# Python-unrolled loops of a four-stage transformer kernel turned into hardware loops

## The reference

```python
x = x + xattn0(ctx, ctx, layernorm(x))        # softmax over ctx·normed x, applied to ctx
x = x + gated_ffn(layernorm(x))               # NF4 weights, 1024 -> 2752 -> 1024, silu(gate) * up
x = x + pooled_gate(layernorm(x), ctx)        # mask of the top 154 of 256 channels of ctx, pools, conv, sigmoid
x = x + fp8_linear(layernorm(x))              # x and weight rounded to fp8, matmul in f32, bias
```

## Time and profile before

| | us |
|---|---|
| three runs | 1971.41, 1971.42, 1970.74 |
| their median | 1971.41 |
| the profiled execution, its own time | 1971.41 |
| its span, first to last instruction | 1969.6 |
| busy in it: PE, DVE, ACT, POOL | 1716.5, 1822.7, 1206.9, 1080.0 |

### The profile page before, as it was taken

How to read it: one execution, slowest core, us unless ns; L and a number is a source line. 1 busy time by engine, 2 the same in 40 slices (tenths; PEclk the granted TensorE clock), 3 DMA queues, 4 the chain that set the end, 5 groups by cost and what they waited for, 6 DMA issues and landing times. The chain is left out here.

```text
span 1969.6 us, 26301 instructions
## 1 busy us (share of the span) xinstructions
PE 1716.5 (87%) x8581; PEld 867.4 (44%) x8720; DVE 1822.7 (93%) x4424; ACT 1206.9 (61%) x1980; POOL 1080.0 (55%) x835
## 2 busy tenths in 40 slices
PE   6997199999999999999999999999999989432656
PEld 4665044444444444444444444444444443232322
DVE  4886799999999999999999999999999997787997
ACT  2442766666675766666756666667566661495754
POOL 2222666566565665655656656566566560255673
PEclk9999599999999999999999999999999999665778
DMA  8343111111111111111111111111111000221212
GB/s 315 118 137 87 25 19 22 20 27 19 22 25 17 23 22 19 26 20 22 24 18 24 22 19 26 20 22 23 18 24 21 15 13 2 86 65 54 65 43 86
DMA packets 96665, 82.59 MB, mean 42 GB/s; under 512 B 35216, under 2 KB 87184, under 8 KB 96528
## 3 DMA queue, kind: packets, MB, share of 16 engines
q1 hardware_dynamic: 60880, 63.99, 10.1%
q0 software_dynamic: 35648, 16.92, 7.3%
HBM read 74.72 MB, written 23.07 MB: 50 GB/s over the span
## 5 line engine op out<-in xcount | busy, mean ns | idle before, releaser
L713 ACT ACTIVATE b_high_line<-code,b_line_bias 128x512 f32<-128x512 bf16 (+2 forms) x528 | 348.7, 707 | 353.8 <-DVE b_weight L873 353.8
L814 PE MATMUL b_up_ps<-xT_high,b_gate_up 128*128 128x512 bf16 x1344 | 413.5, 379 | 0.0
L814 PE MATMUL b_gate_ps<-xT_high,b_gate_up 128*128 128x512 bf16 x1322 | 403.4, 381 | 0.1
L638 POOL TENSOR_TENSOR b_parts<-b_weight,b_parts 128x512 bf16<-128x512 f32 (+1 forms) x132 | 151.9, 1151 | 415.5 <-ACT b_parts L723 415.5
L713 ACT ACTIVATE b_low_line<-code,b_line_bias 128x512 f32<-128x512 bf16 (+2 forms) x528 | 347.5, 706 | 28.8 <-POOL b_high_line L655 27.3
L932 DVE MATCH_REPLACE8 b_left<-b_best,b_left 128x256 f32<-128x256 f32 x832 | 332.9, 404 | 0.0
L915 DVE MAX8 b_best<-b_left 128x8 f32<-128x256 f32 x832 | 308.7, 409 | 0.2
L814 PE MATMUL b_gate_ps<-xT_low,b_gate_up 128*128 128x512 bf16 x703 | 268.2, 381 | 5.1 <-issue 0.9
L814 PE MATMUL b_up_ps<-xT_low,b_gate_up 128*128 128x512 bf16 x672 | 254.7, 379 | 0.0
L647 POOL TENSOR_TENSOR b_low_line<-b_low_line 128x512 f32<-128x512 f32 (+1 forms) x132 | 187.5, 1420 | 102.2 <-ACT b_low_line L713 101.7
L835 PE MATMUL b_down_ps<-b_down,b_inner_high 128*128 128x512 bf16 (+1 forms) x662 | 210.7, 380 | 0.1
(11 more groups left out here) (154 smaller groups left out, 3044.1 us busy)
## 6 DMA issues: line engine op xcount, KB each, us to landing
x_rows<-in_x_dram SPq DMA_DIRECT2D x8, 1024.0 KB, 5.7
a_ctx<-in_ctx_dram SPq DMA_DIRECT2D x8, 1024.0 KB, 6.9
ctx_t<-a_kT SPq DMA_DIRECT2D x8, 1024.0 KB, 7.1
b_left<-ctx_t SPq DMA_DIRECT2D x64, 128.0 KB, 2.2
mask<-mask_t SPq DMA_DIRECT2D x16, 512.0 KB, 3.8
out_dram<-x_rows SPq DMA_DIRECT2D x8, 1024.0 KB, 4.0
code<-in_L_ffn_gate_codes_dram POOLq DMA_DIRECT2D x42, 128.0 KB, 3.1
code<-in_L_ffn_up_codes_dram POOLq DMA_DIRECT2D x42, 128.0 KB, 2.9
```

The source lines that it names most:

```text
L638: nc.gpsimd.tensor_tensor(parts[j % 2][0:a, 1, 0:n], weight[j % 2][0:a, 0:n], parts[j % 2][0:a, 0, 0:n], ALU.subtract).then_inc(low_made, 1)
L713: ins = nc.scalar.activation((low_line, high_line)[side][i][0:a, 0:n], code[slot][0:a, 0:n], ACT.Relu, bias=line_bias[0:a, side, i:i + 1], ...
L814: ins = nc.tensor.matmul(out, gu_w[b][:, which, wp, k, 0:rows], xT[xp][:, k, tg * HW:(tg + 1) * HW], start=(k == 0 and n == 0), stop=(k == ...
```

## The change

Seven `for` loops of Python, which write a copy of the body per pass, become `Fori` loops, which each engine that takes part runs with an index in a register. `Fori` sets the register, runs the body, adds the step and branches back while the index is under the end. Inside, `c`, `i` and `b` are then no Python integers, so that the thresholds of waits, the slices of X and the addresses of DMAs that depend on them are computed on the engine. `at(m, n)` is false and `there(b)` and `reused(b)` are true in a loop, whose passes are those for which that holds.

```diff
 # attention
         def bodies(eng, body):
             body(0, 0, True, False)
-            for i in range(0, B // 2 - 1):
+            with eng.Fori(0, B // 2 - 1) as i:
                 body(2 * i + 1, 1, True, True)
                 body(2 * i + 2, 0, True, True)
 # attention, SP's loads of X
-            for i in range(0, B // 2 - 1):
+            with sp.Fori(0, B // 2 - 1) as i:
                 for p in range(2):
 # gated_ffn
         def chunks(eng, chunk):
-            for c in range(0, CHUNKS - 2):
+            with eng.Fori(0, CHUNKS - 2) as c:
                 chunk(c)
 # pooled
-            for i in range(1, B // 2 - 1):
+            with eng.Fori(1, B // 2 - 1) as i:
                 body(2 * i, 0)
                 body(2 * i + 1, 1)
 # pooled, SP's loads of masks
-            for i in range(0, B // 2 - 1):
+            with sp.Fori(0, B // 2 - 1) as i:
 # gates_and_fp8_ffn
         def rounds(eng, body):
             body(0, 0)
-            for i in range(0, (B - 4) // 2):
+            with eng.Fori(0, (B - 4) // 2) as i:
                 body(2 * i + 1, 1)
                 body(2 * i + 2, 0)
 # gates_and_fp8_ffn, SP's last stores
-            for b in range(B - 5, B):
+            with sp.Fori(B - 5, B) as b:
                 store(b)
```

## The result

| | us |
|---|---|
| before, four runs in all | 1971.08 median, 1970.19 to 1971.42 |
| after, four runs | 2001.48 median, 2000.66 to 2003.20 |
| after, three more on record | 1998.09, 2000.80, 2002.92 |
| ratio after / before | 1.0153, 95% interval 1.0139 to 1.0168 |
| predicted | 2010, range 1978 to 2042 |

A forecast was written before the change was run, and what follows sets the result against it. PE and DVE, both nearly full in each FFN chunk, were taken to bound the kernel. Taken branches (27.4 us) and register values (11.6 us) added 39.0 us to 1971.41, giving 2010 us, range 1978 to 2042.

The forecast's parts named there:

- Full engines, nothing saved by less code: PE and DVE are within 2 us of full in each FFN chunk; fewer instruction fetches save 0.
- PE fetches the head of its body again (2.4 us a chunk in the sum): At each taken FFN branch PE refetches for 3.1 us, 2.7 showing; with DVE alongside, 2.4 was charged.
- rival (a): PE keeps its body, so DVE's stall counts, less its waits for PE: 26.4 us, 1998 in all; chance 0.20.
- far fewer than 69 packets: Sign on PE's instruction queue q8 that would speak for PE keeping its body through the loop.
- passed five blocks ago, so gone: PE looks ahead about one block, so its body's head, passed five blocks ago, must be fetched again.
- DVE fetches (1.7 us shown): At a taken FFN branch DVE's refetch takes 2.7 us, 1.0 covered by queued adds, so 1.7 show.
- ACT's branch under cover: ACT's 2.7 us branch in the FFN falls into time it waits for DVE, so nothing is charged.
- the number of engine instructions stays as it is: Claim for the whole kernel that arithmetic, tiles, order and number of engine instructions and DMAs do not change.
- Registers, 11.6 us: Values computed in registers where an engine has run dry, all stages: 232 x 0.05 us = 11.6 us.
- Branches of the other stages, 8.2 us: Taken branches outside the FFN: 4.8 us in the first stage, 3.4 in the third and fourth.
- the FFN's branches: Eight taken branches of the FFN loop at 2.4 us each: 19.2 us.

The follow-up runs named there:

- kernel 7: The changed kernel with DVE's FFN back edge hinted and a one-column Silu ahead of ACT's chunk: 1972.25 us, 1.0005 of the kernel before.
- kernel 6: The changed kernel with one more ACT operation, a one-column Silu, at the head of each chunk: 1995.32 us, 1.0121 of the kernel before.

## Why the prediction was right, and where it wasn't

Direction and range held: slower, 2001.5 us in 1978 to 2042. The forecast's 2010 was 8.5 us too high, and its parts were off by more than that, in both directions. So the measured time lies near it partly by luck, as said below.

**Full engines, nothing saved by less code.** Right. DVE's busy time is unchanged, straight chunks still take 131.4 us, and the part of the code that is no longer fetched (q8: 47 packets fewer) brought no time. The other engines' queue carries more than before, 75 packets against 68, though their code is shorter too.

**PE fetches the head of its body again (2.4 us a chunk in the sum).** Wrong; this is the step that failed. Between 384 and 1460 us the DMA view of the kernel after has only the other engines' queue, where the kernel before had 43 packets of q8 (after, then before):

```profile
q14 instruction: 48, 0.39, 0.1%
```

```profile
q8 instruction: 43, 0.70, 0.3%
```

PE holds its whole body through the loop, which was rival (a)'s premise, and the prediction had named the sign of it, far fewer than 69 packets. The inference "passed five blocks ago, so gone" took looking ahead by one block for holding only a few. Counted in the trace from branch to branch, sequencer instructions included, PE keeps 1415 instructions and loses 2803.

**DVE fetches (1.7 us shown).** Right in mechanism. The fetch took 2.8 to 3.4 us over eight branches where 2.7 was assumed, and 2.2 us of it shows as idle time. Its worth, measured with ACT straight, is 1.59 us a chunk, 12.7 us in all. Rival (a) had 1.0, since it took off 0.7 us of DVE's waits as waits for PE; of these rows 3 have only 0.4 for PE, the other 0.3 is for ACT. Its 1998 is nearer than the forecast, but it lacks the table loads as well.

**ACT's branch under cover.** The branch is (0.26 us, its code is there). What no term held is that ACT's function tables are loaded twice per pass. By the means they cost 8 x 0.80 = 6.4 us by themselves and 8 x 1.38 = 11.0 us more together with DVE's stall. With 12.7 for the stall that is 30.1 us of the 30.0 of the eight chunks; the terms are differences of the same means, so their sum is no test of them. Firm are the ends: 0.8 us a chunk for the loads without the stall, 2.2 us with it. The diff showed no sign of the loads. The sentence of the prediction that they break is the one by which the number of engine instructions stays as it is: ACT has 1997 against 1980.

**Registers, 11.6 us.** Mis-sized. With every engine looping and both other costs taken away (kernel 7), a chunk takes 0.07 us more than straight, under 0.6 us in the FFN where 72 x 0.05 = 3.6 were charged; all else that the other six loops do costs 0.2 to 3.7 us. The likeliest reason is that the values are computed while the engines have work queued, which the prediction held for most of them and should have held for nearly all; no run isolates it.

**Branches of the other stages, 8.2 us.** Mis-sized. Their bodies stay in place: in attention the first taken branch of line 225 on DVE is at 77.4 us and the next pass begins 0.3 us later, and no taken branch of the loops outside the FFN took more than 0.33 us to the next instruction on any engine. Only 0.5 us are lost ahead of the chunks and 0.5 behind them.

The Trainium skill ("Runtime: NRT & Kernel Launch", Instruction fetch mechanics) says that a taken branch out of a window of two blocks must fetch by DMA. Here PE's body of 1415 instructions, more than five of its blocks, was not fetched again, which goes against the rule. DVE's 488 were. With blocks as small as q14's 8.2 KB, two hold some 256 instructions (an estimate from the 128 a block), which fits DVE but not POOL's 318, which stayed; with the page's 256 instructions a block it would be 512, which fits POOL but not DVE. The list of the Trainium skill that the prediction set beside it ("Advanced Engine Details and Errata", ISA Cache), 128 KB on TensorE and 32 KB elsewhere, fits PE: an estimate from it at 64 bytes an instruction (its 16 KB over its 256 instructions) is 2048, between 1415 and 2803. For the others the same estimate is 512, and here bodies of 488 and 392 were fetched again while 318 stayed, so it is some way too high or a loop can't use all of it.

So the total was near because errors of both signs met: the FFN's branches were charged 6.5 us too much (19.2 for 12.7) and the other branches and the registers some 19 too much (8.2 + 11.6 for about 1), while 17.4 us of table loads were missing. That the range held is owed to the stall, whose mechanism was right on DVE; that its centre lay so near was luck.

## What to carry to other kernels

Turn unrolled code into a loop only after counting each engine's body: it costs when a body doesn't stay in that engine's store, and then about 3 us per pass on that engine, of which 1.6 us showed here on DVE. There a hint on the back edge removed the gap (chunks at 132.3 instead of 135.2 us); on other engines it was not tried. Look in the instruction counts for loads of ACT's function tables that the loop adds, and begin the body with a function whose set serves all of it; with both done all seven loops run at the straight code's time (1.0005, 0.9996 to 1.0014), but none was faster. Where two small delays on different engines come at one point, measure them together: 0.07 us a chunk of one became 0.8 to 1.4 beside the other.

## What the runs showed of the hardware

- A taken branch whose target is in place takes 0.16 to 0.33 us to the next instruction (0.25 to 0.31 in the FFN's loop); one whose code must be fetched takes 2.8 to 3.4 us on DVE, 2.5 to 2.7 on ACT and 3.4 to 3.9 on PE.
- Loops whose bodies stayed, in instructions of one pass: PE 1415, POOL 318, ACT 198, DVE 138 (attention). Fetched again: PE 2803, DVE 488 and 974, ACT 392. This goes by the time from branch to next instruction.
- A load of ACT's function tables takes 1283 ns each time. In straight code the FFN has one; in a loop each pass has two, and one if the pass begins with a Silu. The Trainium skill ("ScalarE activation tables: per-element evaluation and per-set limits", Table sets in the compiler and the runtime) says that the back end places these loads per block; the traces agree, 9 passes with 2 each.
- One hint instruction of 39 ns per pass removed DVE's wait of 3 us; from branch to next instruction it is then 0.5 us (913.1 to 913.6).
- In the changed kernel and kernel 6, DVE's line 861 started while POOL's line 647 ran, and ended 0.55 us after POOL's whenever it had started: it took 1.1 to 1.8 us instead of 0.68.
